# A gated attention block: outputs turned a slot later, projections gathered, values in another bank

## The reference, cut to what matters

```python
def attention(q, k, v):                  # 16 heads of 8 features
    scores = einsum('bqhd,bkhd->bhqk', q * 8 ** -0.5, k)
    return einsum('bhqk,bkhd->bqhd', softmax(scores), v)

x = x + tanh(g_xattn) * attention(layernorm(x), ctx, ctx)
z = layernorm(x)
r = rope(z)
q, k, v = r @ Wq.T + bq, r @ Wk.T + bk, z @ Wv.T + bv
a = causal_attention(q, k, v) @ Wo.T + bo
x1 = layernorm(z + a) * ln1_w + ln1_b
gates = softmax(x1 @ gate_w.T + gate_b)              # the two largest of 8 are kept
moe = sum over the two of gate * (x1 @ expert_w.T + expert_b)
x = x + tanh(g_ffn) * (layernorm(x1 + moe) * ln2_w + ln2_b)
```

## Time and profile before

| | |
|---|---|
| time of three runs | 461.24, 461.83 (median), 461.96 us |
| the profiled execution | 461.55 us, of which the span from first to last instruction is 459.7 us |
| busy share of the span | TensorE 87%, VectorE 82%, GpSimd 70%, ScalarE 60% |
| mean granted TensorE clock | 0.984 of full speed |
| first half, one unit of eight slots | 8.37 us |
| second half, one unit of eight slots | 10.14 us |

### The profile page before, as it was taken

How to read it: one execution, slowest core, us unless ns; L and a number is a source line. 1 busy time by engine, 2 the same in 40 slices (tenths; PEclk the granted TensorE clock), 3 DMA queues, 4 the chain that set the end, 5 groups by cost and what they waited for, 6 DMA issues and landing times.

```text
span 459.7 us, 17611 instructions
## 1 busy us (share of the span) xinstructions
PE 399.5 (87%) x6568; PEld 241.5 (53%) x6568; DVE 375.3 (82%) x1196; ACT 278.0 (60%) x705; POOL 320.1 (70%) x712
## 2 busy tenths in 40 slices
PE   0369888889878899999999999999879999999993
PEld 0235545445445566656666666666545555555542
DVE  6688999999998787878877877775167999999986
ACT  1126777776776666666666666666515666567562
POOL 4466677676698888878888788434743677777783
PEclk9999999999999999999999999999969999999997
DMA  6856696665444443334434443330000000000001
GB/s 163 198 141 167 178 202 168 167 177 131 123 118 116 108 118 98 94 101 108 108 102 115 113 109 96 100 91 14 2 0 1 1 24 24 11 25 18 19 24 46
DMA packets 88036, 42.75 MB, mean 93 GB/s; under 512 B 16000, under 2 KB 87824, under 8 KB 87952
## 3 DMA queue, kind: packets, MB, share of 16 engines
q1 hardware_dynamic: 76544, 38.61, 31.6%
q10 hardware_dynamic: 11408, 3.02, 2.9%
HBM read 5.69 MB, written 2.10 MB: 17 GB/s over the span
## 4 chain that ended last, share of the span: by engine, by line
PE 47%; ACT 5%; DVE 4%; issue 3%; POOL 0%; ACTq 0%; DVEq 0%; POOLq 0%
PE u_bank L445 7%; PE s_bank L804 7%; PE st_bank L804 6%; PE s_bank L383 4%; PE s_bank L396 3%; PE u_bank L822 3%; DVE r L619 2%; PE u_bank L792 2%; PE u_bank L820 2%; ACT z_x_t L871 2%; PE t_bank L375 2%; PE t_bank L369 2%; PE st_bank L396 2%; PE u_bank L458 2%; ACT part L506 1%
## 5 line engine op out<-in xcount | busy, mean ns | idle before, releaser
L638 DVE TENSOR_REDUCE nm<-s_bank 128x4 f32<-128x512 f32 x256 | 171.6, 683 | 37.8 <-PE s_bank L396 34.5
L528 ACT ACTIVATE pt<-st_bank 128x512 f32<-128x512 f32 x256 | 149.3, 601 | 77.1 <-PE u_bank L445 41.1
L396 PE MATMUL s_bank<-qk 64*64 64x128 bf16 (+1 forms) x1536 | 102.5, 221 | 12.2 <-DVE nm L638 6.0
L445 PE MATMUL u_bank<-pt,vaug 128*32 128x128 f32 x2048 | 109.5, 286 | 1.6
L396 PE MATMUL st_bank<-qk 64*64 64x128 bf16 (+1 forms) x1588 | 101.7, 218 | 0.0
L396 PEld LDWEIGHTS s_bank<-qk 64*64 64x64 bf16 (+1 forms) x1536 | 72.9, 104 | 36.2 <-issue 18.9
L396 PEld LDWEIGHTS st_bank<-qk 64*64 64x64 bf16 (+1 forms) x1588 | 72.1, 103 | 0.0
L445 PEld LDWEIGHTS u_bank<-pt,vaug 128*32 128x32 f32 x2048 | 40.8, 108 | 27.2 <-issue 3.8
L383 PE MATMUL s_bank<-mqk,idb 64*64 64x256 bf16 x256 | 38.3, 291 | 2.7 <-ACT pt L528 0.8
L383 PE MATMUL st_bank<-mkq,idb 64*64 64x256 bf16 x256 | 38.3, 293 | 0.1
L292 POOL TENSOR_TENSOR part<-r,part 128x512 bf16<-128x512 f32 x32 | 37.0, 1157 | 1.4
(11 more groups left out here) (129 smaller groups left out, 840.0 us busy)
## 6 DMA issues: line engine op xcount, KB each, us to landing
qk<-part SPq DMA_DIRECT2D x221, 128.0 KB, 2.8
x_all<-x SPq DMA_DIRECT2D x16, 128.0 KB, 2.7
qk<-qrow SPq DMA_DIRECT2D x32, 64.0 KB, 2.1
qk<-mts ACTq DMA_DIRECT2D x64, 32.0 KB, 2.4
c_all<-ctx_in SPq DMA_DIRECT2D x14, 128.0 KB, 2.8
out<-z_o SPq DMA_DIRECT2D x14, 128.0 KB, 1.8
ewt<-exp_t SPq DMA_DIRECT2D x1, 512.0 KB
qk<-part ACTq DMA_DIRECT2D x3, 128.0 KB, 2.6
```

The costliest lines, as they stand in the source:

```text
L396: ins = pe.matmul(to[outs, :], fixed[:, outs], moving, start=not masked, stop=True, skip_group_check=masked)
L445: ins = pe.matmul(u_bank[b][32 * j:32 * j + 32, r * P:(r + 1) * P], v, pt[m % 4][:, j, :], start=half == 0, stop=half == 1, skip_group_che ...
L528: act.activation(pt[m % 4][:, :, :].rearrange("k j q -> k (j q)"), st_bank[m % 2][:, :], ACT.Exp).then_inc(ex, 1)
L638: dve.tensor_reduce(nm[q % 2][:, first:first + HEADS], s_bank[n % 2][:, :].rearrange("q (j k) -> q j k", j=HEADS), AX_X, ALU.max, negate=T ...
```

## The change

The turn of a sequence's output moves one slot later (slots 1 and 5 in place of 0 and 4), and with it the normalise on VectorE (slots 2 and 6 in place of 1 and 5) and the addition to x on GpSimd. In slots 1 and 5 TensorE now turns the output, then the inputs (slot 1, both halves), then the maxima, which stood at the start of slots 2 and 6. The projections of queries, keys and values stand together at the end of slot 3; before, queries and keys were at the end of slot 2 and values at the end of slot 5. The values go through columns 256 to 511 of the bank of the turned maxima (`m_bank`) in place of `t_bank`, with two new waits, and into one of five value buffers. ScalarE's copy of the turned inputs and its high part move from slots 1 and 3 to 2 and 4; on VectorE the rest of the high part moves from slot 4 to 5, the values from 7 to 4, the statistics from 5 to 3; GpSimd's middle and low part and its deviation move as shown. VectorE zeroes the fifth buffer in the first unit.

```diff
-U_TURN = U_COPY + 1
-U_NORM = U_COPY + 2
-U_ADD = U_COPY + 3
+U_TURN = U_COPY + 2
+U_NORM = U_COPY + 3
+U_ADD = U_COPY + 4
+VALUES = 5
...
-        vaug = [sb(f"vaug{i}", [P, G, H, 48]) for i in range(RING)]
+        vaug = [sb(f"vaug{i}", [P, G, H, 48]) for i in range(VALUES)]
...
 # GpSimd
-                    if t == (4 if in_x(s + 2) else 5):
+                    if t == (4 if in_x(s + 2) else 6):
                         middle_part(s + 2)
-                    if t == (5 if in_x(s + 2) else 6):
+                    if t == (5 if in_x(s + 2) else 7):
                         low_part(s + 2)
...
-                if in_y(s + 4) and t == 7:
+                if in_y(s + 4) and t == (4 if in_y(s + 3) else 7):
                     deviation(s + 4)
...
 # TensorE, transpose_inputs
-                if u > GROUPS:
-                    pe.wait_ge(vy, u - GROUPS)
-                elif u >= 1:
+                if u >= 1:
                     pe.wait_ge(r_s, high_parts(u - 1))
...
             def project_v(u):
-                pe.wait_ge(r_s, high_parts(u))
+                pe.wait_ge(mts_s, (u - 2) * G)
                 for b in range(G):
-                    ins = pe.matmul(t_bank[:, b * P:(b + 1) * P], txr[:, (G + b) * P:(G + b + 1) * P], wv[:, :],
+                    ins = pe.matmul(m_bank[:, W + b * P:W + (b + 1) * P], txr[:, (G + b) * P:(G + b + 1) * P], wv[:, :],
                                     start=True, stop=True)
...
 # transpose_max
+                if q % G == 0 and in_y(q // G + 2):
+                    pe.wait_ge(vy, q // G + 2 - GROUPS + 1)
...
 # TensorE's loop
-                q = seq_at(n, 6)
-                if q is not None:
-                    transpose_max(q)
                 tile_n = n if 0 <= n < LAST_TILE else None
...
                 q = seq_at(n, U_TURN)
                 if q is not None:
                     transpose_u(q)
-                if in_x(s + 2) and t == 1:
+                if 0 <= s + 2 < UNITS and t == 1:
                     transpose_inputs(s + 2)
-                if in_y(s + 2):
-                    if t == 0:
-                        transpose_inputs(s + 2)
-                    if t == 2:
-                        project(s + 2)
-                    if t == 5:
-                        project_v(s + 2)
+                q = seq_at(n, 5)
+                if q is not None:
+                    transpose_max(q)
+                if in_y(s + 2) and t == 3:
+                    project(s + 2)
+                    project_v(s + 2)
...
 # ScalarE's loop
                 if in_y(s + 2):
-                    if t == 1:
+                    if t == 2:
                         copy_inputs_t(s + 2)
-                    if t == 3:
+                    if t == 4:
                         high_part(s + 2)
...
 # VectorE's values and loop
-                                  t_bank[:, 0:W].rearrange("k (b h d) -> k b h d", b=G, d=D),
+                                  m_bank[:, W:2 * W].rearrange("k (b h d) -> k b h d", b=G, d=D),
...
+                if n == FIRST_SLOT + 3 * TILES + 2:
+                    value_columns(dve, 4)
-                if in_y(s + 4) and t == 5:
+                if in_y(s + 4) and t == (3 if in_y(s + 3) else 5):
                     statistics(s + 4)
...
                 if in_y(s + 2):
                     if t == 4:
+                        values(s + 2)
+                    if t == 5:
                         rest_of_high(s + 2)
-                    if t == 7:
-                        values(s + 2)
```

More of the change, by code:

```diff
@@ L116, in gated_block_kernel @@
         c_tanh = sem("tanh_ready"); c_half = sem("exponent_set"); c_two = sem("expert_bias_zeroed")
-        c_mst = sem("max_stacks_set"); c_low = [sem(f"lower_set{i}") for i in range(RING)]; c_val = [sem(f"value_columns_set{i}") for i in range(RING)]
+        c_mst = sem("max_stacks_set"); c_low = [sem(f"lower_set{i}") for i in range(VALUES)]; c_val = [sem(f"value_columns_set{i}") for i in range(VALUES)]
         c_late = sem("later_constants_loaded"); c_l2 = sem("last_norm_gated"); c_w = sem("weights_permuted")
@@ L443, in av @@
                     h = 2 * (HEADS * r + j) + half
-                    v = vaug[u % RING][:, b, h, 16 * (1 - half):16 * (1 - half) + 32]
+                    v = vaug[u % VALUES][:, b, h, 16 * (1 - half):16 * (1 - half) + 32]
                     ins = pe.matmul(u_bank[b][32 * j:32 * j + 32, r * P:(r + 1) * P], v, pt[m % 4][:, j, :],
@@ L516, in values @@
                 act.wait_ge(x_in[u % AHEAD], 32 * (u // AHEAD + 1))
-                if u >= RING:
-                    act.wait_ge(av_s, (u - RING + 1) * TILES)
+                if u >= VALUES:
+                    act.wait_ge(av_s, (u - VALUES + 1) * TILES)
                 else:
                     act.wait_ge(c_val[u], 1)
-                act.activation(vaug[u % RING][:, :, :, 16:16 + D],
+                act.activation(vaug[u % VALUES][:, :, :, 16:16 + D],
                                pair(c_all, u).rearrange("k b (h d) -> k b h d", d=D), ACT.Copy).then_inc(vx, 1)
@@ L624, in values @@
                 dve.wait_ge(vproj, u - GROUPS + 1)
-                dve.wait_ge(av_s, (u - RING + 1) * TILES)
-                dve.tensor_tensor(vaug[u % RING][:, :, :, 16:16 + D],
-                                  t_bank[:, 0:W].rearrange("k (b h d) -> k b h d", b=G, d=D),
+                dve.wait_ge(av_s, (u - VALUES + 1) * TILES)
+                dve.tensor_tensor(vaug[u % VALUES][:, :, :, 16:16 + D],
+                                  m_bank[:, W:2 * W].rearrange("k (b h d) -> k b h d", b=G, d=D),
                                   bvb[:, :].rearrange("k (h d) -> k h d", d=D).unsqueeze(1)
```

## The result

The changed kernel takes 481.24 us (median of 4 runs, 478.68 to 482.67) against 461.83: a ratio of 1.042, interval 1.037 to 1.046. The forecast was 479.5. The profiled execution took 481.32 us with a span of 479.2, 19.5 longer than before, at a mean granted clock of 0.977.

A forecast was written before the change was run, and what follows sets the result against it. VectorE was taken to pace the first half, TensorE the second. Second half 9.9, last units 1.3, units between 1.0, first half 4.5 and memset 1.2 sum to 17.9, so 479.5 us; own range 474 to 485, stated range 466 to 486.

The forecast's parts named there:

- The wait that decides: Values product (av) of slots 3 and 7 waits for VectorE's normalise, now directly before it and behind that slot's reduce.
- Its size: Second half: slot 3's av loses 0.53 us, slots 4 to 7 lose 0.69; a unit grows 0.71, fourteen units +9.9.
- TensorE's own work: Second-half unit: 10.14 us less 0.57 idle gives 9.57, taken over unchanged for the changed kernel.
- First half: VectorE loses its gap before the rest but gains two others: net +0.41 us in each of 11 units, +4.5.
- the gaps of 0.60 and 0.25: First half, VectorE: 0.60 us lost at slot 2's reduce, 0.25 through slot 7's av waiting for slot 6's normalise.
- The memset: VectorE zeroes the fifth value buffer in the first unit: +1.2 us, bounds 0 to 1.45.
- At nothing: Parts priced at zero: moved statistics, deviation, middle and low part, output turn's dropped wait, five buffers, shared bank's waits.
- The two waits on the shared bank: Slot 5's maxima turn waits for VectorE's values, the projection for the maxima's copy; both cost nothing, 0.5 us to spare.
- The transition and the end: Two units before the second half, 0.5 us each: +1.0; last two units, without projections, four times 0.33: +1.3.
- the rival that I gave 0.04: The clock: TensorE idles more, one fall of some 10 us costs at most 5, 484.5 us; chance 0.04.
- The one that ends faster: Normalise is ready in time at slot 3's av, and gathering removes both old second-half waits: 454.8 us; chance 0.09.
- ScalarE alone: Av's wait is covered but the inputs' copy is late, 0.59 us at the projection: 467.6 us; chance 0.11.

The follow-up runs named there:

- e3: Changed kernel with VectorE's normalise taken ahead of the maxima (reduce) of the same slot; 466.58 us.
- e5: Changed kernel with the fifth value buffer's memset moved ahead of the first tile, where VectorE waits for GpSimd; 478.98 us.
- e9: Changed kernel with normalise and addition back in the slots of the kernel before, only the output's turn a slot later; 466.72 us.
- e6: Changed kernel with the outputs' turn, normalise and addition each one more slot later; 563.71 us.
- e4: e3 with ScalarE's copy of the turned inputs ahead of its copy of the maxima in slot 2; 458.25 us.
- e10: e8 with turn, normalise and addition back in the slots of the kernel before; 456.82 us.
- e8: Changed kernel with normalise, slot 4's values and rest ahead of maxima, inputs' copy ahead of maxima's, high part ahead of exponential, memset earlier; 451.42 us.

## Why the prediction was right, point by point

*The wait that decides.* Right in place, releaser and order: the av of slots 3 and 7 waits for the product, in 57 of the 62 sequences whose av asks for a normalise. e3 shows it: the normalise moved by one reduce takes 14.7 us away (the clock's part included), with the same work on every engine.

*Its size.* Near, and in part by luck. Slot 3 was predicted to lose 0.53 and slot 7 0.69; the idle times in the rows are 0.55 and 0.81. Counted as the prediction counts, from the start of the slot's scores (247.06 and 242.07) plus 0.45, the losses are 0.62 and 0.89. The term that was too small is the signal from the product to the av: 0.06 in the prediction, from the rest of the high part and the projection of the values, but 0.14 and 0.15 here (the products end at 247.99 and 243.26). In slot 7 TensorE is also there 0.09 earlier. The other way, TensorE's own work was taken over as 9.57 and is 10.79 - 0.62 - 0.89 = 9.28: steps that now stand next to one another take less. Queries, keys and values projected in a row take 1.51 us (248.49 to 250.00); apart they took 1.06 and 0.55, the first as these rows of the kernel before show:

```profile
233.12 0.70 PE L369 MATMUL t_bank<-txr,wqp 128*128 128x256 f32 x2
...
234.18 0.29 PE L383 MATMUL s_bank<-mqk,idb 64*64 64x256 bf16 x1
```

The turn of the second output takes 0.28 (240.83 to 241.11) and took 0.37, and the turns of the inputs save as much again. So the losses were 0.23 too small, the saving of 0.29 was left out, and the two errors cancel: a unit was to grow by 0.71 and grew by 0.64, 9.0 in place of 9.9 over 14 units.

*First half.* +0.41 predicted, +0.40 measured, and this was luck in part as well. With the overlap of 0.08 that the prediction counts in, the gaps of 0.60 and 0.25 were 0.61 and 0.42: the second was 0.17 too small, again by the longer signal (0.15, from 89.70 to 89.85) and by an overlap. About as much was saved at a place where the prediction had nothing. In the kernel before, VectorE in the stretch of the earlier trace rows had short waits that the view doesn't mark:

```profile
88.92 0.35 DVE L655 SCALAR_TENSOR_TENSOR ao<-u_bank,tg,rec 128x128 f32<-128x128 f32 x1
89.25 1.38 DVE L638 TENSOR_REDUCE nm<-s_bank 128x4 f32<-128x512 f32 x2
```

The first reduce here starts 0.33 after the product and not 0.27, as in the changed kernel; the two last 1.38 and not 1.28. These waits, some 0.17 a unit, are gone after the change.

*The memset.* 1.2 predicted, 1.5 measured: the upper bound. Nothing hid it where it was put.

*At nothing.* The two waits on the shared bank cost nothing: the view of waits has no line in which TensorE's turn of the maxima waits for the values, or `project_v` for the copy of the maxima.

*The transition and the end.* The four units around the change of halves became longer by 5.2 us in the changed kernel and by 2.9 in e5, whose other units are the same. I had 1.0 for two of them and counted the others as the first half's, 0.8, so 1.8. The difference of 2.2 between the two kernels I put down to the clock, the one thing in which these units are seen to differ. Busy time by stretch of the changed kernel (the clock behind the busy times) and, last, of e5:

```profile
131.00:134.00 3.00, 1.93 (x39) 1.02 (x35) 2.90 (x13) 2.29 (x9) 2.71 (x5) 1.00 0.48 122
137.00:143.50 6.50, 6.21 (x80) 3.24 (x78) 4.70 (x13) 3.71 (x9) 5.87 (x14) 0.52 0.18 47
154.00:157.00 3.00, 1.68 (x39) 1.06 (x40) 2.63 (x7) 1.99 (x6) 1.96 (x3) 0.98 0.37 98
157.00:160.60 3.60, 3.60 (x43) 2.23 (x41) 1.69 (x4) 1.15 (x4) 3.21 (x9) 0.54 0.64 168
```

```profile
129.60:132.60 3.00, 1.93 (x39) 1.02 (x35) 2.89 (x13) 2.29 (x9) 2.71 (x5) 1.00 0.38 95
```

Twice TensorE was at the lower level, 1.2 GHz (0.52 and 0.54 of full speed), a little after a stretch with 1.93 and 1.68 us busy of 3.00. The kernel before shows 1.00 from 120 to 180 us, and so does e5, though its stretch at 129.60 is as busy as the one at 131.00, with the same 39 matmuls: such a stretch alone doesn't decide, and what does, no run here shows. The runs agree: the changed kernel's run of 478.68 us had a mean clock of 0.987, those of 481.16 to 482.67 had 0.974 to 0.977. So the rival that I gave 0.04 came on top of the forecast in three of four runs, at 2.2 us in the profiled one in place of 5. At the end nothing is left of the 1.3 that I added: the normalise was 19.7 us late at the start of unit 27, 20.8 two units later and 19.9 at the last sequence, and the span is 19.5 longer.

The sum, term by term (us; measured in the profiled executions):

| term | predicted | measured |
|---|---|---|
| second half, 14 units | 9.9 | 8.8 |
| four units around the change of halves | 1.8 | 5.2 (2.2 of it the clock) |
| first half, 9 units | 3.7 | 3.5 |
| memset | 1.2 | 1.5 |
| first normalise, a slot later (e5) | 0 | 0.65 |
| end | 1.3 | -0.2 |
| sum | 17.9 | 19.5 |

Two terms were too large (the second half and the end), three too small or left out (the four units, the first normalise, the clock), and they about cancel: the changed kernel's run with the mean clock of 0.987 took 478.68, 0.8 under the forecast. The mechanism was right; that the time came so near is partly luck.

*The rivals.* The one that ends faster fell at the point that I had named: the signal came at 0.55 after TensorE was there, not before. ScalarE alone was real, and hidden: e3 comes near to this rival's kernel, with a second-half unit 0.20 longer than before where it gave 0.22, and 466.6 us where it gave 467.6 (the first half, where it gave 0.16 a unit, lost nothing). By the Trainium skill (PSUM — Partial Sum Buffer, section on bank collisions), which has two engines on one bank and quadrant in the same cycle raise an error, the av's wait is needed. No run here takes it away and tests that; e3 and e9 show that it may stay as it is and cost next to nothing, if the normalise comes earlier (av of slot 7: 0.21 in e3).

*Not tried:* the fifth buffer and the shared bank apart. With four buffers the values in slot 4 would need an av that comes in slot 6.

## What to carry to other kernels

When a step is delayed by a slot, look for counts that other engines wait for with a fixed distance: a wait that the diff doesn't touch can lose its slack and tie two engines together in one slot. Price the wait from the place in the queue of the awaited instruction, not from its slot: here one reduce ahead of it, which could as well go behind, was worth 14.7 us, the clock's part included. Work whose input is there belongs in front of an instruction whose input comes late (the memset, the values, the high part), and small TensorE steps of one kind next to one another.

## What the runs showed of the hardware

TensorE's clock can fall again and again though no idle time is longer than 1.7 us: in e6, between 40 and 234 us, it fell 15 times, to a mean of 0.78 of full speed, with waits of 1.42 us twice a unit. Between 235 and 320 us, with waits of 1.36 us twice in 12.5 us, it stayed at 1.00; what makes the difference no run here shows. The Trainium skill (TensorE: Matmul & The Clock Gate, section on the clock's oscillation in real kernels) tells of a kernel whose clock falls anew with every wait for a DMA; e6 agrees in part, with waits on another engine, of which about every second one up to 234 us, and few after that, were followed by a fall (mean clock over the whole kernel 0.899).

The signal from a VectorE instruction to a TensorE one that waits for it took 0.06 us before the projection of the values (237.29 to 237.35 in the kernel before) and 0.14 to 0.15 before an av (247.99 to 248.13 in the changed one).

A DMA that ScalarE issues holds its queue for 0.54 us (240.87 in e4), nearly as long as the copy of 128x512 beside it (0.60); what stands behind it comes that much later.

Turns and projections that follow one another save 0.05 to 0.10 us each time against the same ones apart (a turn of an output 0.27 for 0.37, the projections 1.51 for 1.61). In a unit that TensorE paces this is gain: 0.24 of the 0.27 between e10 and e8 (two outputs 0.10 and 0.09, the inputs 0.05).
